# Top-64 attention on one Trainium2 core: the scan of candidates one step later, marks held twice, and GpSimd's pass over the scores

## The chip, the cores and the metric

The kernel runs on one core of one Trainium2 chip. The metric is device time in microseconds of one launch. The engines are TensorE (PE in the profile, PEld for its weight loads), VectorE (DVE), ScalarE (ACT), GpSimd (POOL) and SyncE (SP). A name with a q behind it (DVEq) is the sequencer of that engine, which handles waits, registers and branches.

## The reference

Sixteen batches of 512 rows of width 128 go through one layer of attention with 16 heads and a feed-forward layer. What matters here is the attention's choice of keys:

```
dots = einsum('bhid,bhjd->bhij', q, k) * scale     # 16 memory keys + 512 keys
dots = einsum('bhij,hk->bkij', dots, pre_proj)     # heads mixed
dots = where(causal, -max, dots)
vk   = top_k(dots, 64)[0][..., -1:]                # the 64th largest of each row
attn = softmax(where(dots < vk, -max, dots))
attn = einsum('bhij,hk->bkij', attn, post_proj)
out  = einsum('bhij,bhjd->bhid', attn, v) @ Wo + bo
x = x + layernorm(out);  x = x + layernorm(ffn(layernorm(x)))   # silu-gated ffn
```

## The kernel before

The kernel works in steps of one head of one batch: `step(s)` for s from 0 to 15, sixteen batches, and a "drain" batch at the end; a loop holds two batches. `g` counts the steps over all batches. A head's scores are four row tiles t = 3, 2, 1, 0 of 528, 400, 272 and 144 columns (only keys that the mask allows), 1344 columns in all, in one of 8 ring slots of `scores`.

To find the 64th largest value of each row, the kernel doesn't sort. It guesses a threshold, counts how many scores lie above it, moves the guess by a secant step, and repeats three times, once a step. A head goes through these stages, each on its own lag behind the step in which its scores are made:

- lag 0: TensorE makes the scores (L713 and L715, the causal mask added as a matmul); VectorE takes them out of PSUM (L1061, semaphore `masked`).
- lags 1, 2, 3: ScalarE counts with `Sign` (`count(k)`, L871, four tiles each, semaphore `counted[k]`). VectorE moves the three guesses in flight at once (the guess block, L1123 to L1149, semaphore `guess_ready`).
- lag 4 (`LAG_K`): VectorE counts a last time and writes marks 0 or 1 into `work` (`count_found`, L1014). It then writes score - FMAX * mark over them in one pass of 1344 columns (L1080), scans for the 8 largest that are left (MAX8, L1092) and picks the wanted one by its rank (`pick_rank` L1099 and `pick_value` L1107, semaphore `kth_ready`); GpSimd makes the table of ranks for that (`offset`, L1260, semaphore `offset_ready`). ScalarE takes the exponentials (L892). Rows for which the number found was too far off are counted (`spread` L1078, `missed` L1084, semaphore `bad_ready`).
- the flags: TensorE sums `missed` over partitions (L761, place ("FLAG", s) in the `misc` banks), ScalarE copies the sum to `flags` (L803, near the end of its step), and VectorE, one step later, loads it into a register (`value_load`, L1029). If it isn't zero, VectorE works out the tile concerned exactly (`general_kth`, L987 to L995).
- lag 5 (`LAG_P`): VectorE applies threshold and exponentials (L1048) and takes the reciprocal of the row sum (L1053, semaphore `rinv_ready`); GpSimd scales (L1269, `scaled`), TensorE transposes (L737, `turn`), ScalarE copies (L882, `take_turned`).
- lag 6 (`LAG_V`): TensorE weighs the values (L724).

Nothing is scheduled by a planner: each engine runs its own hand-written order and waits on semaphores. ScalarE's order in a step is `count(2)`, `count(1)`, `take_extra(0)`, the copy of G for the next head, `count(0)`, `take_extra(1)`, then the turned tiles between the exponentials, and the flag. The "extras" are projections, the feed-forward layer and the like, put into the steps by the table `EXTRAS`; their PSUM banks `misc` alternate, and `misc_free` counts every copy out of them in a fixed order. The two lines that tie the engines together around the change are, for ScalarE and VectorE:

```
L866  at_least(act, first_ready if k == 0 else guess_ready, g if k == 0 else g - 1)
L1028 dve.wait_ge(misc_free, flag_index(kind, b, s) + 1)   # ("FLAG", s - 1) has been copied
```

`guess_ready` goes up by one with each guess block. Before the change the block of VectorE's step g brings it to g, so `count` in ScalarE's step g (which wants g - 1) needs the block of step g - 1.

GpSimd's order in a step is `negmax` (L1249), the seed of a new guess (L1255), `offset` (L1260), the four scalings (L1269), `pmem` (L1276), the memory keys' scores (L1285), then its extras: layer norms (L1194 to L1204), residual sums (L1210) and a product of the feed-forward layer (L1307).

Of the kernel before, what the change touches and what calls it, by code (L numbers as in the profile page):

```python
# [41 lines left out]
MASKED = -2.0 ** 100  # L42
# [14 lines left out]
LAG_P = 5  # L57
LAG_V = 6
# [18 lines left out]
          4: [("U", 7), ("U", 8)],  # L77
          5: [("PM", 0), ("PM", 1)],
          6: [("U", 9), None],
          7: [("MEM", 0), ("MEM", 1)],  # L80
          8: [("U", 10), ("X1T",)],
          9: [("GATE", 0), ("UP", 0)],
          10: [("GATE", 1), ("UP", 1)],
          11: [("GATE", 2), ("UP", 2)],
          12: [("U", 11), ("U", 12)],
          13: [("DOWN", 0), ("DOWN", 1)],
          14: [("U", 13), ("U", 14)],
          15: [("U", 15), None]}
# [15 lines left out]
def guess_table():  # L104
# [23 lines left out]
    for t in range(T):  # L128
        for i in range(P):
# [4 lines left out]
            table[i, t] = z  # L134
            table[i, T + t] = z - FAR / (2 * density)
# [13 lines left out]
def flagged(kind, s):  # L149

    return lagged(kind, s, LAG_K)
# [120 lines left out]
def build(nc, table, x, wq, wk, wv, pre, post, memk, memv, wo, bo, wgate, wup, wdown, out):  # L272
    with ExitStack() as ctx:  # L273
# [12 lines left out]
        work = sb("work", [P, WIDE])  # L286
# [39 lines left out]
        found = sb("found", [P, T])  # L326
# [18 lines left out]
        minus_one = sb("minus_one", [P, T])  # L345
# [72 lines left out]
        found_ready = sem("found_ready")  # L418
        offset_ready = sem("offset_ready")
# [141 lines left out]
        def _(pe):  # L561
# [179 lines left out]
            def batch(kind, b, par):  # L741
                def step(s):
# [20 lines left out]
                    if lagged(kind, s, LAG_P):  # L763
                        turn(head_of(s, LAG_P), g - LAG_P, 2)
# [9 lines left out]
        def _(act):  # L774
# [20 lines left out]
            for q in range(4):  # L795
                nc.scalar.mul(a_all[:, 4 * q:4 * q + 4, :], banks[q][:, :].rearrange("p (h n) -> p h n", h=4),
                              DH ** -0.5).then_inc(a_taken, 1)
            nc.scalar.mul(amem[:, :, :], banks[4][:, 0:H * M].rearrange("p (h n) -> p h n", h=H),
                          DH ** -0.5).then_inc(a_taken, 1)
# [29 lines left out]
            def batch(kind, b, par):  # L829
                def step(s):  # L830
# [54 lines left out]
                    def exponentials(p):  # L885

                        if lagged(kind, s, LAG_K):
                            ge, t = g - LAG_K, ORDER[p]
# [3 lines left out]
                            nc.scalar.activation(row(expo, ring(head_of(s, LAG_K), ERING), t),  # L892
                                                 row(scores, ring(head_of(s, LAG_K), RING), t), ACT.Exp,
                                                 bias=negmax[:, bass.ds(ring(head_of(s, LAG_K), RING), 1), t]
# [31 lines left out]
        def _(dve):  # L926
# [76 lines left out]
            def batch(kind, b, par):  # L1003
                def step(s):
# [25 lines left out]
                    if selects:  # L1030
                        count_found(ORDER[2])
                        count_found(ORDER[3])
# [313 lines left out]
```

## Time and profile before

| what | us |
|---|---|
| median of 3 runs | 3636.93 (3633.64 to 3641.19) |
| the profiled execution's own time | 3636.07 |
| its span, first to last instruction | 3634.3 |
| VectorE busy | 3292.4 (91% of the span) |
| ScalarE busy | 3199.3 (88%) |
| TensorE matmuls busy | 2795.9 (77%) |
| GpSimd busy | 1551.4 (43%) |

The span is the time between the first and the last instruction in the trace; the profiled execution took 1.8 us more than its span. Busy time is the union of an engine's instructions; idle time is put down to what released the engine. One step takes some 13.5 us, and each engine does about the same in every step, so most of the reading is done on one step.

### The profile page before, as it was taken

How to read it: one execution, taken by the hardware profiler on the slowest of the kernel's cores; microseconds unless marked ns; L12 is line 12 of the kernel's file. 1: busy time of each engine (PE TensorE's matmuls, PEld its weight loads, DVE VectorE, ACT ScalarE, POOL GpSimd, SP SyncE). 2: the span in 40 equal slices, each digit the busy share in tenths (PEclk: the TensorE clock that was granted, in tenths of full speed). 3: DMA queues.
4: the chain of work that ended last, by engine and by line, in shares of the span. 5: the costliest groups of instructions: out<-in, count | busy, mean ns of one | idle time of the engine just before them, and what ended most of it. 6: DMA issues, size and time to landing. Idle time of an engine off the chain costs nothing. (4 is left out here: it accounts for less than half of the span.)

```text
span 3634.3 us, 67348 instructions
## 1 busy us (share of the span) xinstructions
PE 2795.9 (77%) x13751; PEld 1808.7 (50%) x13751; DVE 3292.4 (91%) x12492; ACT 3199.3 (88%) x9018; POOL 1551.4 (43%) x2663
## 2 busy tenths in 40 slices
PE   7777778777777878778778867877777788877765
PEld 3455455545545545555455545544555455545544
DVE  4699999999999999999999999999999999999994
ACT  1799999999979999999999979998999999999973
POOL 3233444444434444444444444443444444444433
PEclk9888999988888899888998888899889998899886
DMA  1000000000000000000000000000000000000000
GB/s 41 7 2 2 5 8 5 8 2 5 8 4 8 5 8 2 5 8 5 8 5 7 2 4 8 5 8 2 5 8 5 8 5 8 2 5 8 2 7 4
DMA packets 31375, 22.37 MB, mean 6 GB/s; under 512 B 3201, under 2 KB 30338, under 8 KB 30722
## 3 DMA queue, kind: packets, MB, share of 16 engines
q1 hardware_dynamic: 30722, 16.03, 1.6%
q14 instruction: 532, 4.36, 0.4%
q8 instruction: 121, 1.98, 0.2%
HBM read 11.83 MB, written 4.19 MB: 4 GB/s over the span
## 5 line engine op out<-in xcount | busy, mean ns | idle before, releaser
L871 ACT ACTIVATE signs<-scores,state 128x528 int8<-128x528 f32 (+3 forms) x3072 | 1764.3, 574 | 181.8 <-DVE state L1149 103.4
L713 PE MATMUL s_bank<-xn,gT 128*128 128x512 f32 (+3 forms) x2048 | 900.6, 568 | 1.7 <-issue 0.7
L1269 POOL TENSOR_SCALAR probs<-probs,rinv 128x528 f32<-128x528 f32 (+3 forms) x1024 | 547.1, 553 | 507.3 <-DVE rinv L1053 507.3
L737 PE MATMUL t_bank<-ident,probs 128*128 128x128 f32 x2560 | 482.7, 313 | 299.1 <-POOL probs L1269 289.7
L724 PEld LDWEIGHTS y_bank<-u_all,probsT 128*128 128x128 f32 x5120 | 619.9, 194 | 133.4 <-issue 124.2
L724 PE MATMUL y_bank<-u_all,probsT 128*128 128x128 f32 x5120 | 625.2, 278 | 7.1 <-ACT probsT L882 7.1
L1260 POOL TENSOR_TENSOR offset<-consts,found 128x36 f32<-128x36 f32 x256 | 161.7, 632 | 1047.5 <-DVE work L1014 1047.5
L871 ACT ACTIVATION_READ_ACCUMULATOR signs<-scores,state 128x1 f32 x3072 | 575.7, 187 | 0.0
L737 PEld LDWEIGHTS t_bank<-ident,probs 128*128 128x128 f32 x2560 | 299.7, 153 | 506.8 <-issue 398.6
L1048 DVE SCALAR_TENSOR_TENSOR probs<-scores,kth,expo 128x528 f32<-128x528 f32 (+3 forms) x1024 | 522.8, 565 | 24.8 <-issue 19.1
L892 ACT ACTIVATE expo<-scores,negmax 128x528 f32<-128x528 f32 (+3 forms) x1024 | 535.0, 575 | 0.0
L1014 DVE TENSOR_SCALAR_CACHE_REDUCE work<-scores,state 128x528 f32<-128x528 f32 (+3 forms) x1024 | 515.5, 559 | 20.2 <-issue 12.3
L1061 DVE TENSOR_SCALAR_CACHE_REDUCE scores<-s_bank,memmax 128x512 f32<-128x512 f32 (+3 forms) x1024 | 502.5, 547 | 3.8 <-PE s_bank L715 3.4
L713 PEld LDWEIGHTS s_bank<-xn,gT 128*128 128x128 f32 x2048 | 393.4, 239 | 222.4 <-issue 212.3
L882 ACT COPY probsT<-t_bank 128x512 f32<-128x512 f32 (+1 forms) x768 | 390.6, 509 | 104.5 <-PE t_bank L737 102.7
L1092 DVE MAX8 state<-work 128x8 f32<-128x528 f32 (+3 forms) x1024 | 444.9, 500 | 0.0
L1080 DVE SCALAR_TENSOR_TENSOR work<-work,scores 128x1344 f32<-128x1344 f32 x256 | 404.9, 1582 | 0.0
L599 PE MATMUL misc<-b_all,xn 128*128 128x512 f32 x512 | 281.3, 631 | 50.5 <-ACT u_all L803 46.3
L1276 POOL COPY pmem<-probs 128x64 f32<-128x64 f32 x256 | 303.5, 1186 | 35.9 <-issue 2.5
L761 PE MATMUL misc<-missed,onesP 128*1 128x5 f32 x512 | 49.4, 168 | 343.0 <-DVE missed L1084 340.0
L634 PE MATMUL misc<-xn,a_all 128*128 128x512 f32 x512 | 263.2, 596 | 0.0
L715 PE MATMUL s_bank<-causal,ident 128*128 128x128 bf16 x1024 | 250.5, 245 | 0.0
(148 smaller groups left out, 3384.9 us busy)
## 6 DMA issues: line engine op xcount, KB each, us to landing
xwork<-in_L_attn_x_dram SPq DMA_DIRECT2D x17, 256.0 KB, 2.8
xres<-in_L_attn_x_dram SPq DMA_DIRECT2D x16, 256.0 KB, 2.9
out_dram<-ybuf SPq DMA_DIRECT2D x16, 256.0 KB, 2.4
u_all<-in_L_attn_Wq_dram SPq DMA_DIRECT2D x1, 512.0 KB, 3.7
u_all<-in_L_attn_Wk_dram SPq DMA_DIRECT2D x1, 512.0 KB, 4.5
u_all<-in_L_attn_Wv_dram SPq DMA_DIRECT2D x1, 512.0 KB, 5.3
u_all<-in_L_attn_Wo_dram SPq DMA_DIRECT2D x1, 512.0 KB
expo<-in_L_ffn_w_gate_dram SPq DMA_DIRECT2D x1, 192.0 KB, 4.7
```

The source lines that it names most:

```text
L713: nc.tensor.matmul(score_part(t, 0, KEYS[t]), lhsT=gT[s % 2][:, t * P:(t + 1) * P], rhs=xn[par][:, 0:KEYS[t]], start=True, stop=False, ski ...
L724: mm = nc.tensor.matmul(y_bank[:, t * P:(t + 1) * P], lhsT=probsT[:, h % 2, at:at + P], rhs=u_all[:, j, h * D:(h + 1) * D], start=False, s ...
L737: mm = nc.tensor.transpose(t_bank[q % 2][:, at:at + P], probs[:, h % 2, KEY_AT[t] + j * P:KEY_AT[t] + (j + 1) * P], ident[:, :])
L871: nc.scalar.activation(signs[:, k, 0:ROW[t]], row(scores, ring(head_of(s, k + 1), RING), t), ACT.Sign, bias=guesses(s % STATES, k, GUESSES ...
L882: nc.scalar.copy(probsT[:, h % 2, PART_AT[q]:PART_AT[q + 1]], t_bank[q % 2][:, 0:PART_AT[q + 1] - PART_AT[q]]).then_inc(t_taken, 1)
L892: nc.scalar.activation(row(expo, ring(head_of(s, LAG_K), ERING), t), row(scores, ring(head_of(s, LAG_K), RING), t), ACT.Exp, bias=negmax[: ...
L1014: v.tensor_scalar(work[:, AT[t]:AT[t] + ROW[t]], row(scores, slot_k, t), guessed[:, t:t + 1], None, ALU.is_ge, ALU.add, accum_out=found[:, ...
L1048: v.scalar_tensor_tensor(out=probs[:, slot_p % 2, AT[t]:AT[t] + ROW[t]], in0=row(scores, slot_p, t), scalar=kth[:, bass.ds(slot_p, 1), t], ...
L1061: v.tensor_scalar(keys(scores, slot, t), score_part(t, 0, KEYS[t]), 1.0, memmax[par][:, t, bass.ds(s, 1)], ALU.mult, ALU.max, accum_out=ro ...
L1080: v.scalar_tensor_tensor(out=work[:, :], in0=work[:, :], scalar=-FMAX, in1=scores[:, bass.ds(slot_k, 1), :].squeeze(1), op0=ALU.mult, op1= ...
L1092: v.max(candidates(now)[:, t, 1:9], work[:, AT[t]:AT[t] + ROW[t]]).then_inc(select_step, 1)
L1269: nc.gpsimd.tensor_scalar(prb, prb, rinv[:, slot_p, t:t + 1], 1.0, ALU.mult, ALU.mult).then_inc(scaled, 1)
```

## The change

Three parts:

1. The lags. Applying moves from lag 5 to 6 (`LAG_P`), the values from 6 to 7 (`LAG_V`), the exponentials and flags get a lag of their own, 5 (`LAG_E`). The scan for candidates (MAX8) and the pick run one step after the marks were made; so `work` and `found` are held twice.
2. The pass over 1344 columns leaves VectorE. GpSimd does it as four subtractions, score - mark, one for each tile. So that a subtraction of 1 is enough to push a marked score under all others, all scores are scaled by 2^-60, and the scale is taken back in the exponential.
3. The order on VectorE. A step now begins with scan and pick, then the check of the number found, the feed-forward product, the guess block, one `count_found`, the applying, the other three `count_found`, and the scores out of PSUM. On ScalarE the flag comes after the last turned tile, on TensorE after the third `turn`.

```diff
-MASKED = -2.0 ** 100
+UNIT = 2.0 ** -60
+MASKED = -2.0 ** 40
...
 LAG_K = 4
-LAG_P = 5
-LAG_V = 6
+LAG_E = 5
+LAG_P = 6
+LAG_V = 7
...
-        work = sb("work", [P, WIDE])
+        work = sb("work", [P, 2, WIDE])
-        found = sb("found", [P, T])
+        found = sb("found", [P, 2, T])
...
 (TensorE)
                     if lagged(kind, s, LAG_P):
-                        turn(head_of(s, LAG_P), g - LAG_P, 0)
-                        turn(head_of(s, LAG_P), g - LAG_P, 1)
+                        for q in range(3):
+                            turn(head_of(s, LAG_P), g - LAG_P, q)
                     if flagged(kind, s):
-                        pe.wait_ge(bad_ready, g - LAG_K + 1)
+                        pe.wait_ge(bad_ready, g - LAG_E + 1)
...
-                    if lagged(kind, s, LAG_P):
-                        turn(head_of(s, LAG_P), g - LAG_P, 2)
...
 (ScalarE)
                     exponentials(2)
                     exponentials(3)
+                    take_turned(2)
                     if flagged(kind, s):
-                        at_least(act, probs_ready, 4 * (g - LAG_K))
+                        at_least(act, probs_ready, 4 * (g - LAG_E))
                         take(kind, b, par, ("FLAG", s), flags[:, :], ...)
-                    take_turned(2)
...
 (VectorE, at the start of a step)
+                    if applies:
+                        dve.wait_ge(hidden, 4 * gp + 4)
+                        alone(dve)
+                        for p, t in enumerate(ORDER):
+                            if p == 2:
+                                dve.wait_ge(misc_free, flag_index(kind, b, s) + 1)
+                                alone(dve)
+                                rows_missed = dve.value_load(flags[0:1, T:T + 1].bitcast(I32), ...)
+                            v.max(candidates(past)[:, t, 1:9], work[:, s % 2, AT[t]:AT[t] + ROW[t]]).then_inc(select_step, 1)
+                        dve.wait_ge(offset_ready, gp + 1)
...
                     if moves:
                         for k in range(GUESSES):
-                            if lagged(kind, s, k + 1):
-                                dve.wait_ge(counted[k], 4 * (g - k))
+                            if lagged(kind, s, k + 2):
+                                dve.wait_ge(counted[k], 4 * (g - k - 1))
...
-                        v.tensor_tensor(guesses(soon, 1, GUESSES), guess, move[:, :], ALU.subtract).then_inc(guess_ready, 1)
+                        v.tensor_tensor(guesses(now, 1, GUESSES), guess, move[:, :], ALU.subtract).then_inc(guess_ready, 1)
...
-                        v.scalar_tensor_tensor(out=work[:, :], in0=work[:, :], scalar=-FMAX,
-                                               in1=scores[:, bass.ds(slot_k, 1), :].squeeze(1),
-                                               op0=ALU.mult, op1=ALU.add).then_inc(select_step, 1)
...
 (GpSimd)
+                    if lagged(kind, s, LAG_K):
+                        gk, slot_k = g - LAG_K, ring(head_of(s, LAG_K), RING)
+                        for p, t in enumerate(ORDER):
+                            pool.wait_ge(found_ready, 4 * gk + p + 1)
+                            alone(pool)
+                            wrk = work[:, s % 2, AT[t]:AT[t] + ROW[t]]
+                            nc.gpsimd.tensor_tensor(wrk, row(scores, slot_k, t), wrk, ALU.subtract).then_inc(hidden, 1)
```

The wait of `count` on `guess_ready` (L866) isn't edited. The block of VectorE's step g now brings `guess_ready` to g - 1, since the first block runs one step later.

VectorE, in the middle of a batch, before: from the end of the guess block to the load of the flag (`candidates` are part of `state`, and `flags` holds what ScalarE copied in its last step).

```order
L1149 TENSOR_TENSOR state<-state,move 128x12
L1092 MAX state<-work 128x8 [waits select_step]
L1092 MAX state<-work 128x8 x3
L1099 SCALAR_TENSOR_TENSOR offset<-offset,state 128x4x9 [waits select_step,offset_ready]
L1106 ISA [waits select_step]
L1107 TENSOR_REDUCE kth<-offset 128x4
L1014 TENSOR_SCALAR work,found<-scores,state 128x528 [waits masked,guess_ready,mem_placed]
L1014 TENSOR_SCALAR work,found<-scores,state 128x400
L1029 TENSOR_LOAD flags [waits misc_free]
L1029 ISA x2
L1014 TENSOR_SCALAR work,found<-scores,state 128x272
L1014 TENSOR_SCALAR work,found<-scores,state 128x144
```

The same engine after the change, from the start of a step to the start of the guess block.

```order
L1031 MAX state<-work 128x8 [waits hidden]
L1031 MAX state<-work 128x8
L1029 TENSOR_LOAD flags [waits misc_free]
L1029 ISA x2
L1031 MAX state<-work 128x8 x2
L1034 SCALAR_TENSOR_TENSOR offset<-offset,state 128x4x9 [waits select_step,offset_ready]
L1038 ISA [waits select_step]
L1039 TENSOR_REDUCE kth<-offset 128x4
L1046 SCALAR_TENSOR_TENSOR spread<-found 128x4 [waits found_ready]
L1049 SCALAR_TENSOR_TENSOR missed<-spread,consts 128x4 [waits select_step]
L1069 TENSOR_TENSOR state<-counts,consts 128x12 [waits first_ready,counted2,counted0,counted1]
```

The load of the flag stood behind the guess block of the step before and some half a step ahead of the next one; it now stands directly ahead of a guess block, with two scans, the pick and the check between them.

ScalarE after the change, over the end of a step and the start of the next one.

```order
L883 COPY probsT<-t_bank 128x512 [waits t_full]
L893 ACTIVATE expo<-scores,negmax 128x272
L893 ACTIVATE expo<-scores,negmax 128x144
L880 REGISTER_ALU
L883 COPY probsT<-t_bank 128x256 [waits t_full]
L803 REGISTER_ALU [waits probs_ready]
L804 COPY flags<-misc 1x5 [waits misc_full]
L872 ACTIVATE signs,counts<-scores,state 128x528 [waits mem_placed,counted2,masked,guess_ready]
```

The copy of the flag was the last but one instruction of a step and is now the last; the next step still opens with `count(2)`, which waits for the guess.

GpSimd after the change, from the start of a step.

```order
L1237 TENSOR_TENSOR negmax<-rowmax,minus_unit 128x4 [waits masked]
L1243 COPY state<-seed 128x2x4 [waits guess_ready]
L1252 COPY scores<-smem 128x2x32 [waits probs_ready]
L1258 TENSOR_TENSOR offset<-consts,found 128x4x9 [waits kth_ready,found_ready]
L1268 TENSOR_SCALAR probs<-probs,rinv 128x528 [waits rinv_ready,probs_ready]
L1268 TENSOR_SCALAR probs<-probs,rinv 128x400
L1268 TENSOR_SCALAR probs<-probs,rinv 128x144
L1268 TENSOR_SCALAR probs<-probs,rinv 128x272
```

Behind these come the four subtractions and `pmem`, and then the extras; the memory keys' copy has moved ahead of `offset`.

## Rows read from the trace of the kernel before

**Rows 1.** The page, busy time and share of the span by engine.
```profile
PE 2795.9 (77%) x13751; PEld 1808.7 (50%) x13751; DVE 3292.4 (91%) x12492; ACT 3199.3 (88%) x9018; POOL 1551.4 (43%) x2663
```

**Rows 2.** VectorE's waits, 300 to 3500 us: total us, times, longest.
```profile
DVE state L1123 <- ACT signs L871: 0.4, 1, 0.4
```

**Rows 3.** ScalarE's groups, 500 to 3500 us: busy, mean ns, idle before by releaser.
```profile
L871 ACT ACTIVATE signs<-scores,state 128x272 int8<-128x272 f32 (+1 forms) x2667 | 1531.7, 574 | 156.4 <-DVE state L1149 88.1 <-issue 1.1
...
L882 ACT COPY probsT<-t_bank 128x512 f32<-128x512 f32 (+1 forms) x666 | 339.0, 509 | 64.4 <-PE t_bank L737 63.1
L803 ACT COPY gT<-misc 128x512 f32<-128x512 f32 x223 | 130.9, 587 | 5.7 <-PE misc L634 5.7
```

**Rows 4.** Timeline of VectorE, one step: start us, duration us.
```profile
2013.38 0.43 DVE L1078 SCALAR_TENSOR_TENSOR spread<-found 128x4 f32<-128x4 f32 x1
2013.73 1.55 DVE L1080 SCALAR_TENSOR_TENSOR work<-work,scores 128x1344 f32<-128x1344 f32 x1
2015.20 0.19 DVE L1084 SCALAR_TENSOR_TENSOR missed<-spread,consts 128x4 f32<-128x4 f32 x1
...
2015.32 0.25 DVE L1123 TENSOR_TENSOR state<-counts,consts 128x12 f32<-128x12 f32 x1
...
2017.16 1.74 DVE L1092 MAX8 state<-work 128x8 f32<-128x528 f32 x4
2019.01 0.22 DVE L1099 SCALAR_TENSOR_TENSOR offset<-offset,state 128x36 f32<-128x36 f32 x1
2019.37 0.20 DVE L1107 TENSOR_REDUCE kth<-offset 128x4 f32<-128x40 f32 x1
```

**Rows 5.** Timeline of ScalarE, the end of the same step and the next.
```profile
2016.86 0.14 ACT L803 COPY flags<-misc 1x5 f32<-1x5 f32 x1
2016.91 0.37 ACT L882 COPY probsT<-t_bank 128x256 f32<-128x256 f32 x1
2017.28 0.73 ACT L871 ACTIVATE signs<-scores,state 128x528 int8<-128x528 f32 x1
```

**Rows 6.** Timeline of VectorE and ScalarE while the pipeline fills.
```profile
132.60 0.17 DVE L1123 TENSOR_TENSOR state<-counts,consts 128x12 f32<-128x12 f32 x1 [6.92 <-ACT signs L871]
...
134.27 0.17 DVE L1149 TENSOR_TENSOR state<-state,move 128x12 f32<-128x12 f32 x1
134.48 0.73 ACT L871 ACTIVATE signs<-scores,state 128x528 int8<-128x528 f32 x1 [1.53 <-DVE state L1149]
134.62 0.76 DVE L1014 TENSOR_SCALAR_CACHE_REDUCE work<-scores,state 128x528 f32<-128x528 f32 x1 [0.17 <-DVE state L1149]
```

**Rows 7.** Line 1029, the load of the flag: ns min/median/max.
```profile
L1029 DVEq TENSOR_LOAD <-flags x256: 302/306/552, 148.1 to 3580.4; - x128
L1029 DVEq FUSED_REGOPS  x256: 183/199/203, 148.7 to 3580.8; - x128
```

**Rows 8.** GpSimd: two stretches of its timeline and one group by shape.
```profile
2011.69 2.10 POOL L1269 TENSOR_SCALAR probs<-probs,rinv 128x528 f32<-128x528 f32 x4 [2.33 <-DVE rinv L1053]
2013.93 1.45 POOL L1276 COPY pmem<-probs 128x64 f32<-128x64 f32 x1
...
2215.08 0.24 POOL L1276 COPY pmem<-probs 128x64 f32<-128x64 f32 x1
...
2216.07 1.44 POOL L1194 TENSOR_SCALAR vareps<-meanvar 128x4 f32<-128x4 f32 x1 [0.58 <-DVE meanvar L962]
...
2221.21 1.27 POOL L1210 TENSOR_TENSOR ybuf<-xres,ybuf 128x512 f32<-128x512 f32 x1
...
L1307 POOL TENSOR_TENSOR f_up<-f_up,f_gate 128x512 f32<-128x512 f32 x48 | 61.6, 1283 | 8.8 <-ACT f_up L803 8.8
```

**Rows 9.** VectorE's product of the feed-forward layer, by shape.
```profile
L1165 DVE SCALAR_TENSOR_TENSOR f_up<-f_tanh,f_up 128x512 f32<-128x512 f32 x48 | 33.1, 690 | 17.4 <-POOL f_up L1307 15.2 <-issue 2.2
```

**Rows 10.** Timeline behind one `general_kth`: VectorE applies, GpSimd scales.
```profile
2156.32 0.77 DVE L1048 SCALAR_TENSOR_TENSOR probs<-scores,kth,expo 128x528 f32<-128x528 f32 x1 [0.15 <-DVE kth L995]
...
2158.77 2.10 POOL L1269 TENSOR_SCALAR probs<-probs,rinv 128x528 f32<-128x528 f32 x4 [17.97 <-DVE rinv L1053]
```

More of the change, by code:

```diff
@@ L133, in guess_table @@
             active = n + M > TOPK
[L134 to L135 removed]
+            table[i, t] = z * UNIT ** 0.5
+            table[i, T + t] = (z - FAR / (2 * density)) * UNIT ** 0.5
             table[i, 5 * T + 9 * T + t] = float(active)
@@ L149, in flagged @@
 def flagged(kind, s):
-    return lagged(kind, s, LAG_K)
+    return lagged(kind, s, LAG_E)
 def makes_g(kind, s):
@@ L418, in build @@
         found_ready = sem("found_ready")
+        hidden = sem("hidden")
         offset_ready = sem("offset_ready")
@@ L1006, in step @@
                     v = nc.vector
-                    slot_k, slot_p = ring(head_of(s, LAG_K), RING), ring(head_of(s, LAG_P), RING)
-                    gk, gp = g - LAG_K, g - LAG_P
-                    selects, applies = lagged(kind, s, LAG_K), lagged(kind, s, LAG_P)
-                    moves = any(lagged(kind, s, k + 1) for k in range(GUESSES))
-                    now, soon, past = s % STATES, (s + 1) % STATES, (s - 1) % STATES
-                    def count_found(t):
-                        v.tensor_scalar(work[:, AT[t]:AT[t] + ROW[t]], row(scores, slot_k, t), guessed[:, t:t + 1],
-                                        None, ALU.is_ge, ALU.add, accum_out=found[:, t:t + 1]).then_inc(found_ready, 1)
+                    slot_k, slot_e, slot_p = [ring(head_of(s, lag), RING) for lag in (LAG_K, LAG_E, LAG_P)]
@@ new lines, in step @@
+                    gk, ge, gp = g - LAG_K, g - LAG_E, g - LAG_P
+                    selects, checks, applies = [lagged(kind, s, lag) for lag in (LAG_K, LAG_E, LAG_P)]
+                    moves = any(lagged(kind, s, k + 2) for k in range(GUESSES))
+                    now, last, past = s % STATES, (s - 1) % STATES, (s - 2) % STATES
+                    def count_found(t):
+                        v.tensor_scalar(work[:, s % 2, AT[t]:AT[t] + ROW[t]], row(scores, slot_k, t), guessed[:, t:t + 1],
+                                        None, ALU.is_ge, ALU.add,
+                                        accum_out=found[:, s % 2, t:t + 1]).then_inc(found_ready, 1)
@@ new lines, in step @@
+                    if checks:
+                        number = found[:, (s - 1) % 2, :]
+                        dve.wait_ge(found_ready, 4 * ge + 4)
+                        alone(dve)
+                        v.scalar_tensor_tensor(out=spread[:, :], in0=number, scalar=-2.0 * AIM, in1=number,
+                                               op0=ALU.add, op1=ALU.mult).then_inc(select_step, 1)
+                        dve.wait_ge(select_step, 1)
+                        v.scalar_tensor_tensor(out=missed[:, 0:T], in0=spread[:, :], scalar=WINDOW ** 2 + 0.5 - AIM ** 2,
+                                               in1=active, op0=ALU.is_gt, op1=ALU.mult,
+                                               accum_out=missed[:, T:T + 1]).then_inc(bad_ready, 1)
@@ L1053, in step @@
                         v.reciprocal(rinv[:, slot_p % 2, :], rowsum[:, :]).then_inc(rinv_ready, 1)
+                    if selects:
+                        for t in ORDER[1:]:
+                            count_found(t)
                     if kind != "drain":
@@ L1063, in step @@
                                             accum_out=rowmax[:, bass.ds(slot, 1), t]).then_inc(masked, 1)
-                    if s == 6 and kind != "first":
+                    if s == 0 and kind in ("first", "mid"):
+                        dve.wait_ge(x_in, 16 * (b + 2))
+                        norm_stats(kind, b, "x", xwork)
+                    if s == 8 and kind in ("first", "mid"):
+                        memory_maxima(kind, b, 1 - par)
+                    if s == LAG_V and kind != "first":
```

229 lines of the change are left out of this document (99 added, 130 removed).

## The prediction

> **What bounds the kernel now.** I read the page's shares first: VectorE is busy for 91% of the span and ScalarE for 88%, GpSimd for 43% [rows 1]. Then the waits: from 300 to 3500 us VectorE waits for ScalarE's counts 0.4 us in all [rows 2], so it runs nearly without a pause and sets the pace. ScalarE from 500 to 3500 us makes 223 steps (one copy of G each), which is 3000 / 223 = 13.45 us a step; it waits 88.1 us for guesses, 63.1 us for turned tiles and 5.7 us for G [rows 3]. Without these 157 us its step would take (3000 - 157) / 223 = **12.75 us**. So ScalarE is the next bound, 0.7 us behind VectorE.
>
> Last the timelines, for what stands in series. Before the change VectorE's guess block of step g waits for the counts of ScalarE's step g and serves its step g + 1. ScalarE meanwhile does its extras, exponentials and turned tiles. In the step shown the block begins at 2015.32, and ScalarE begins to count at 2017.28, right behind its last copy [rows 4, 5]. The flag, copied at 2016.86, is wanted only in VectorE's next step, ahead of a guess block that serves the step after that. So the loop through the flag spans two steps and doesn't bind.
>
> **The change, part by part.**
>
> The pass over 1344 columns leaves VectorE: 2015.20 - 2013.73 = 1.47 us a step [rows 4]. With it goes a wait at `spread`, which takes 0.43 us there for four columns. If VectorE still set the pace this would give up to 1.7 us, of which only 13.45 - 12.75 = 0.7 us is to be had before ScalarE binds. I book nothing of it, for the next part.
>
> **The flag's wait now stands inside a loop of one step.** In the new order VectorE's step g scans two tiles, waits until ScalarE has copied the flag of step g - 1, loads it, scans two more tiles, picks, checks, and only then runs its guess block. That block now works on the counts of step g - 1 and brings `guess_ready` to g - 1, which is the very value that the first count of ScalarE's step g waits for. And the flag is now the last thing that ScalarE does in a step. So ScalarE ends step g - 1, stands still until VectorE has gone from the flag's load to the end of the guess block, and begins step g. The period is ScalarE's whole step plus this link, whatever VectorE has saved. The link, piece by piece:
> - flag copied to load issued: 0.04 us, as between the end of the guess (134.27 + 0.17) and ScalarE's start at 134.48 [rows 6];
> - the load 0.31 and the register work 0.20, with the assertion behind it 0.55 [rows 7]. Now it stands hidden behind running counts; in the new place nothing is queued, so all of it shows. Bounds: 0.3 (the load alone) and 0.8 (load and register work start 0.6 us apart in the first instance, then 0.2);
> - 0.07 to the scan, then the scans of 272 and 144 columns. Four scans take 1.74 us [rows 4]; by columns the two would be 416 / 1344 of that, 0.54, and half of it would be 0.87. I take 0.64, nearer to the columns, as most of an instruction's time grows with them;
> - scan's end (2017.16 + 1.74) to pick 0.11, taken as 0.10, pick to threshold 0.36 (2019.01 to 2019.37), and 0.23 for the threshold up to the next instruction [rows 4];
> - check: 0.21 for `spread` (bounded by 0.12 and by the 0.35 from 2013.38 to 2013.73), and 0.12 from `missed` at 2015.20 to the guess block [rows 4];
> - the guess block 1.84, from 132.60 to 134.44, and 0.04 to ScalarE [rows 6].
>
> Sum: 0.04 + 0.55 + 0.07 + 0.64 + 0.10 + 0.36 + 0.23 + 0.21 + 0.12 + 1.84 + 0.04 = **4.20 us**, with 3.8 and 5.0 as bounds.
>
> The load, by its rows, isn't slow. The Trainium skill (DMA: Bandwidth & Descriptors, Latency and other measured facts) gives a `tensor_load` a floor of some 600 ns. The rows show 302 ns at least, so they speak against it; by the page the sum would be 0.3 us a step, some 75 us in all, longer.
>
> ScalarE's step itself grows by 0.09: the flag's 0.14 us overlapped the turned tile (2016.86 to 2016.91) and now ends the step [rows 5]. 12.75 + 0.09 = 12.84. I expect no other wait in it. GpSimd begins to scale some 3.5 us after a step's guess, and ScalarE wants the first turned tile behind three counts, 1531.7 / 223 = 6.9 us without their gaps [rows 3], and three copies: some 9 us after it. The two extra slots and G are as before. TensorE has 17 us for what now takes it 2796 / 256 = 10.9 at most. Its wait for `missed` goes, and costs nothing either way.
>
> GpSimd's step. The pass: a product of two tiles of 512 columns takes 1.28 us [rows 8], 2.5 ns a column, so 1344 columns are 3.4 us, with gaps of 0.12 3.85 us (bounds: 2.1 us, the price of the four one-operand scalings, and 5). Counted from the guess's end: VectorE goes on at 0.18 [rows 6], counts one tile (0.7, and 0.2 to the next), applies and takes the reciprocal, and GpSimd starts to scale 2.45 us after the applying began [rows 10], at 3.5; it scales until 5.65, passes until 9.5, copies `pmem` until 9.85. `pmem` takes 0.24 us instead of 1.45, since the latter was a wait beside VectorE's pass [rows 8]. Four small operations lead to `offset` at 11.1. VectorE wants it at 12.84 + 0.04 + 0.55 + 0.07 + 0.64 + 0.10 = 14.2: hidden, with 3 us to spare. Behind the extras it isn't. The norm with residual takes some 5.2 us (2216.07 to 2222.48, less the 1.2 by which its first operation was held up) [rows 8]; it puts `offset` at 16.3, 2.1 us late, twice a batch. The norm without the residual, 1.3 us shorter, makes it 0.8 us late, twice. That is 5.8 us a batch, 0.36 us a step; bounds 0 and 0.8. The feed-forward product on VectorE (0.69 us, three times a batch [rows 9]) now stands between flag and guess: 0.13 us a step.
>
> `general_kth` runs four times as before (the scale is a power of two). It delays the scaling by some 16 us (GpSimd waits 17.97 instead of 2 [rows 8, 10]). Scaling begins at 3.5 and the turned tile is wanted at 9, with a tile's scaling and turning between, so about 5 us of it hide in ScalarE's step now, and it costs three times 11 and once, for a narrow tile, 5: 38 us. The old pace of 13.45 holds such stalls already; I add the 38 nevertheless, since the new pace is without any.
>
> **Sum.** Period 12.84 + 4.20 + 0.36 + 0.13 = **17.53 us**, against 13.45: 4.08 more. The loop closes from step 6 of the first batch into the fourth step of the drain, 253 times: 253 x 4.08 = 1032. With 38: 1070. The profiled execution took 3636.1 us by itself, a microsecond from the median of 3636.9; 3636 + 1070 = 4706, and I write **4700 us**. The lag that the values gain falls into the drain, which has spare steps; I book nothing for it.
>
> **The rivals.**
>
> *The pass comes late or collides.* If GpSimd's loop (scaling, pass, `offset`, pick, guess, applying) were the longer one, it would decide. It takes 11.1 to `offset` against 14.2, so it decides once the pass takes over 7 us. For it: GpSimd and VectorE do hold each other up, as `pmem` (1.45 for 0.24) beside VectorE's pass and `spread` (0.43) beside the last scaling show [rows 4, 8]. Against it: from 5.65 to 9.5 VectorE does counts, evictions and scans, then waits for the flag; the small operations with two operands lie behind 14.2, when GpSimd is idle. The Trainium skill (SBUF - State Buffer, Who interferes with whom) has the rule: a VectorE instruction with two SBUF inputs and a GpSimd instruction that reads SBUF exclude each other. By that rule the pass is undisturbed here. With a pass of 9 us the period would be 2 us longer: 4700 + 506 = 5200 us.
>
> *The flag doesn't bind, GpSimd does.* If the change didn't close the loop as I read it (the flag's wait met early), GpSimd's loop would set the pace: 11.1 to `offset`, and 0.36 + 0.23 + 0.21 + 0.12 + 1.84 = 2.8 plus 0.2 back to the guess's end, 14.1 us. Its extras, 22 us a batch (twice 5.2, twice 3.9, three times 1.3), add 1.4: 15.5 us, 3636 + 253 x 2.05 = 4155 us. Against it: the wait for the flag of step g - 1 is met by one copy alone, since `misc_free` counts in a fixed order.
>
> *Faster.* VectorE's saved pass counts in full, and ScalarE runs without a pause at 12.84 us: 3636 - 253 x 0.61 = 3480 us. Its place is ScalarE's first count of a step; it decides only if the link shrinks to under 0.6 us, or the guess comes a step ahead, and if GpSimd's loop stays under 12.8. The rows speak against both: the guess block alone takes 1.84.
>
> **How the numbers follow.** My forecast, the loop through the flag, gets 0.92; the late pass 0.02, GpSimd's loop without the flag 0.03, not slower 0.03. The range: link at 3.8, no lateness of `offset` and no stalls give 12.75 + 3.8 + 0.13 = 16.7 us, 4455; link at 5.0 and lateness 0.8 give 18.8 us, 5027. All unknowns at one end together are unlikely; half way to the ends holds 8 in 10: 4570 to 4880. A measurement of this kernel tells 0.2% from no change. So faster by more than that 0.02 and within it 0.01, which share the 0.03 of the rival above, and slower 0.97, the other three.
>
> **What would show it.** ScalarE idles some 4.2 us before its first `Sign` of nearly every step, released by the last instruction of the guess block, and hardly elsewhere; its busy time is as before. VectorE idles some 4 to 5 us between the second and the third MAX8 of a step, its busy time lower by some 400 us, 256 passes of 1.55. The link from flag to first `Sign` is 4.2 us. GpSimd's four subtractions take 3.4 us, `pmem` 0.24, `spread` under 0.2; GpSimd idles before the scaling. TensorE no longer waits for `missed`. It would be wrong if ScalarE ran from the flag straight into the count, if the pass met VectorE's small operations, or if VectorE waited mostly for `offset`.

## The result, and the profile after

The changed kernel takes 4640.84 us (median of four executions), the kernel before 3638.12 us beside it: a ratio of 1.276, with a 95% interval from 1.273 to 1.278. The forecast was 4700 us, in a range from 4570 to 4880. One of the four executions took 7459.95 us, at a granted clock of 1.0; it is left out of the ratio, and what happened in it stays open.

The page of the changed kernel, span and shares [rows 1 before]:

```profile
span 4638.8 us, 70407 instructions
...
PE 3121.9 (67%) x13751; PEld 2029.2 (44%) x13751; DVE 2789.2 (60%) x12236; ACT 3188.9 (69%) x9018; POOL 1980.1 (43%) x3687
```

VectorE lost 503 us of work, ScalarE kept its own, and no engine is busy for 70% of the span any more. When all shares fall and the time grows, the time lies in waits. These are the longest of each of the three engines, 500 to 4500 us (total us, times, longest) [rows 2, 3 before]:

```profile
ACT signs L872 <- DVE state L1095: 1047.5, 229, 9.7
ACT probsT L883 <- PE t_bank L740: 29.2, 10, 11.2
ACT smem L804 <- PE misc L645: 10.0, 8, 1.5
...
DVE state L1031 <- ACT flags L804: 1231.2, 228, 6.6
...
DVE offset L1034 <- POOL offset L1258: 34.0, 22, 5.5
...
POOL probs L1268 <- DVE rinv L1124: 2236.2, 230, 26.2
```

In 229 steps ScalarE waits 229 times for the end of the guess block (L1095), 4.57 us each, and VectorE 228 times for the flag, 5.4 us each. Each waits for the other, once a step. The timeline shows one turn of the loop: ScalarE's first count of a step, the end of that step, the link (VectorE's work from the flag to the end of the guess block), and the first count of the next step [rows 4 to 6 before]:

```profile
2501.34 0.73 ACT L872 ACTIVATE signs<-scores,state 128x528 int8<-128x528 f32 x1 [5.03 <-DVE state L1095]
...
2507.75 1.19 DVE L1031 MAX8 state<-work 128x8 f32<-128x528 f32 x2
...
2513.58 0.37 ACT L883 COPY probsT<-t_bank 128x256 f32<-128x256 f32 x1
2513.83 0.15 ACT L804 COPY flags<-misc 1x5 f32<-1x5 f32 x1
2514.72 0.66 DVE L1031 MAX8 state<-work 128x8 f32<-128x272 f32 x2 [5.78 <-ACT flags L804]
2515.49 0.22 DVE L1034 SCALAR_TENSOR_TENSOR offset<-offset,state 128x36 f32<-128x36 f32 x1
2515.85 0.19 DVE L1039 TENSOR_REDUCE kth<-offset 128x4 f32<-128x40 f32 x1
2515.96 0.16 DVE L1046 SCALAR_TENSOR_TENSOR spread<-found 128x4 f32<-128x4 f32 x1
2516.16 0.16 DVE L1049 SCALAR_TENSOR_TENSOR missed<-spread,consts 128x4 f32<-128x4 f32 x1
...
2516.37 0.17 DVE L1069 TENSOR_TENSOR state<-counts,consts 128x12 f32<-128x12 f32 x1
...
2518.04 0.17 DVE L1095 TENSOR_TENSOR state<-state,move 128x12 f32<-128x12 f32 x1
2518.24 0.74 ACT L872 ACTIVATE signs<-scores,state 128x528 int8<-128x528 f32 x1 [4.26 <-DVE state L1095]
```

ScalarE works from 2501.34 to 2513.98, 12.64 us. Then VectorE alone works until 2518.21, and ScalarE starts at 2518.24: a link of 4.26 us. VectorE had been done with its first two scans at 2508.94 and stood still for 5.78 us.

GpSimd in the same step [rows 8 before]:

```profile
2504.92 2.10 POOL L1268 TENSOR_SCALAR probs<-probs,rinv 128x528 f32<-128x528 f32 x4 [10.07 <-DVE rinv L1124]
2506.99 3.47 POOL L1276 TENSOR_TENSOR work<-scores,work 128x528 f32<-128x528 f32 x4
2510.39 0.25 POOL L1283 COPY pmem<-probs 128x64 f32<-128x64 f32 x1
...
2511.03 0.26 POOL L1258 TENSOR_TENSOR offset<-consts,found 128x36 f32<-128x36 f32 x1
```

The pass takes 3.47 us and ends before the flag is there.

### The profile page after: what moved, and what is told of

It is laid out like the page before. It is cut to its first block and busy times, and to the rows that moved or that the text cites. A ratio compares the mean times of both kernels' runs of the same rounds, so it can differ in the third digit from the quotient of the medians.

```text
span 4638.8 us, 70407 instructions
## 1 busy us (share of the span) xinstructions
PE 3121.9 (67%) x13751; PEld 2029.2 (44%) x13751; DVE 2789.2 (60%) x12236; ACT 3188.9 (69%) x9018; POOL 1980.1 (43%) x3687
## 5 line engine op out<-in xcount | busy, mean ns | idle before, releaser
L1031 DVE MAX8 state<-work 128x8 f32<-128x528 f32 (+3 forms) x1024 | 472.2, 506 | 1376.0 <-ACT flags L804 1363.5
L716 PE MATMUL s_bank<-xn,gT 128*128 128x512 f32 (+3 forms) x2048 | 944.2, 589 | 5.9 <-ACT gT L804 4.2
L740 PE MATMUL t_bank<-ident,probs 128*128 128x128 f32 x2560 | 589.5, 385 | 465.0 <-ACT probsT L883 290.2
L1276 POOL TENSOR_TENSOR work<-scores,work 128x528 f32<-128x528 f32 (+3 forms) x1024 | 886.0, 897 | 16.4 <-DVE work L1017 16.4
L602 PE MATMUL misc<-b_all,xn 128*128 128x512 f32 x512 | 381.2, 835 | 622.6 <-ACT u_all L804 480.0
L740 PEld LDWEIGHTS t_bank<-ident,probs 128*128 128x128 f32 x2560 | 451.5, 201 | 747.3 <-issue 352.0
L727 PE MATMUL y_bank<-u_all,probsT 128*128 128x128 f32 x5120 | 649.2, 285 | 10.2 <-ACT probsT L883 10.2
L602 PEld LDWEIGHTS misc<-b_all,xn 128*128 128x128 f32 x512 | 98.0, 240 | 664.8 <-ACT u_all L804 499.6
L696 PE MATMUL misc<-x1T,wgT 128*128 128x512 f32 x96 | 88.6, 1021 | 215.0 <-ACT f_up L804 138.7
L718 PEld LDWEIGHTS s_bank<-causal,ident 128*128 128x128 bf16 x1024 | 117.6, 115 | 159.3 <-issue 133.7
```

What stands on the lines that cost most here:

```text
L602: nc.tensor.matmul(misc[misc_place(kind, par, ("U", u))][:, :], lhsT=xn[par][:, (u % 4) * P:(u % 4 + 1) * P], rhs=b_all[:, 4 * (u // 4):4 ...
L716: nc.tensor.matmul(score_part(t, 0, KEYS[t]), lhsT=gT[s % 2][:, t * P:(t + 1) * P], rhs=xn[par][:, 0:KEYS[t]], start=True, stop=False, ski ...
L727: mm = nc.tensor.matmul(y_bank[:, t * P:(t + 1) * P], lhsT=probsT[:, h % 2, at:at + P], rhs=u_all[:, j, h * D:(h + 1) * D], start=False, s ...
L740: mm = nc.tensor.transpose(t_bank[q % 2][:, at:at + P], probs[:, h % 2, KEY_AT[t] + j * P:KEY_AT[t] + (j + 1) * P], ident[:, :])
L1031: v.max(candidates(past)[:, t, 1:9], work[:, s % 2, AT[t]:AT[t] + ROW[t]]).then_inc(select_step, 1)
L1276: nc.gpsimd.tensor_tensor(wrk, row(scores, slot_k, t), wrk, ALU.subtract).then_inc(hidden, 1)
```

## The experiments

Theory A in all of them: the loop from the flag through VectorE's link to ScalarE's count sets the pace. The rivals are named in each expectation. The edits are made to the changed kernel; `LOAD` stands for the wait on `misc_free`, the nop and the `value_load` of the flag.

**1. The load behind all four scans.**

```diff
                         for p, t in enumerate(ORDER):
-                            if p == 2: LOAD
                             v.max(...)
+                        LOAD
                         dve.wait_ge(offset_ready, gp + 1)
```

> The changed kernel, with VectorE's wait for the flag and its load put behind all four scans instead of between the second and the third. Theory A, the loop through the flag: the two small scans leave the link between flag and guess. In the changed kernel's timeline they and the gap before the pick take 0.66 + 0.1 us, so a step gets some 0.7 us shorter: 4641 - 253 x 0.7 = 4460 us, and ScalarE's idle time before its first count falls from 4.6 to 3.9 us a step. Theory B, GpSimd sets the pace (scaling, pass, ranks): nothing of its chain moves, 4641 us. Theory C, TensorE's lower granted clock (0.79 against 0.88) makes the time: no change, 4641 us.

Measured: 4493.26 us. In plain steps ScalarE's wait is 3.56 us, which is the 4.26 less 0.70:

```profile
1953.95 0.73 ACT L872 ACTIVATE signs<-scores,state 128x528 int8<-128x528 f32 x1 [3.56 <-DVE state L1094]
```

The pick now starts 0.81 us behind the end of the flag's copy, and it was 1.51 us (2513.98 to 2515.49): the same 0.70 us have left the link. The time fell by 148 us and not by 180. Over all steps from 500 to 3500 us ScalarE's wait fell from 4.60 to 4.06 us, by 0.54, since in some steps GpSimd's ranks now come last, after the flag. VectorE's waits that ended with the ranks, over the whole run, changed kernel and this one:

```profile
DVE offset L1034 <- POOL offset L1258: 36.1, 24, 5.5
DVE offset L1033 <- POOL offset L1257: 313.1, 63, 6.0
```

The 313 us are whole waits, most of which would have gone to the flag in any case; what counts is that 63 steps end on the ranks, and it was 24. Theory A holds; B and C, which saw no change, fall.

**2. The flag early.** TensorE sums the flag ahead of the three `turn`s, ScalarE copies it behind `take_extra(1)`.

```diff
                     take_extra(1)
+                    if flagged(kind, s): at_least(...); take(kind, b, par, ("FLAG", s), ...)
                     take_turned(0)
...
                     take_turned(2)
-                    if flagged(kind, s): at_least(...); take(kind, b, par, ("FLAG", s), ...)
```

> The changed kernel, with the flag summed by TensorE ahead of the turned tiles and copied by ScalarE behind its second extra, some 3.1 us earlier in its step; VectorE's order is untouched. Theory A: ScalarE's start to the end of the flag is then 9.6 us, and with a link of 4.26 us the loop through the flag takes 13.9 us instead of 17.5. The steps in which GpSimd does its norms are longer, since its own chain (offset 10 us after ScalarE's start, then 2.8 us to the end of the guess, plus 5.2 us for a norm with residual, 3.9 for one without) comes next: 0.85 us a step on average. 14.75 us against 13.45 before: 3638 + 253 x 1.3 = 3970 us. Theory B: 4641 us, as GpSimd's order is the same. Theory C: 4641 us.

Measured: 4035.04 us. Nothing on VectorE or GpSimd has moved, no work was saved, and 606 us are gone: a copy of 0.15 us, and the matmul that feeds it, had only to come earlier. That is 65 us more than the 3970 expected. A plain step, from count to count in the rows below, is shorter than expected, 13.40 us for 13.9, but the mean is 3000 / 199 = 15.1 us: the steps with GpSimd's norms cost more than the 0.85 us a step booked for them. 63 of VectorE's waits now end on the ranks (500 to 3500 us):

```profile
1948.88 0.74 ACT L872 ACTIVATE signs<-scores,state 128x528 int8<-128x528 f32 x1 [1.19 <-DVE state L1095]
1962.28 0.74 ACT L872 ACTIVATE signs<-scores,state 128x528 int8<-128x528 f32 x1 [1.18 <-DVE state L1095]
...
DVE offset L1034 <- POOL offset L1258: 185.8, 63, 5.9
```

**3. The load late.** `missed` is held twice here, since the wait for the flag had also kept it from being written again too early.

```diff
-                            if p == 2: LOAD
...
                         count_found(ORDER[0])
                     if applies:
+                        LOAD
                         dve.wait_ge(exp_ready, 4 * gp + 4)
```

> The changed kernel, with the wait for the flag and its load behind the guess block and the first count, just ahead of the applying; missed is held twice, so that the earlier wait isn't needed to protect it. Theory A: the flag no longer stands ahead of the guess, the link is gone. What is left is ScalarE's 12.8 us, and GpSimd's chain of 12.7 us in a plain step and 21 us of extras a batch: 14.2 us a step at most, 3638 + 253 x 0.73 = 3820 us, and 3480 us if the extras hide. Theory B: GpSimd's chain is the same, 4641 us. Theory C: 4641 us.

Measured: 4087.31 us. The loop through the flag is open, and the time is far from 3820. The waits say what stands there instead (total us, times, longest, 500 to 3500 us):

```profile
ACT signs L872 <- DVE state L1090: 488.4, 196, 9.2
...
DVE offset L1029 <- POOL offset L1257: 541.5, 195, 5.9
DVE probs L1118 <- issue: 208.1, 201, 3.4
```

VectorE waits in 195 of 196 steps for GpSimd's ranks, which stand behind pass and norms. This is the second rival of the prediction, the GpSimd loop without the flag, to which it gave 15.5 us a step and 4155 us; 3000 / 196 = 15.3 us are measured. The expectation of 3820 had left out what the last row shows: the load, with nothing queued ahead of it, now shows in front of the applying, 1.0 us a step, and that is a piece of GpSimd's loop.

That the rival's 15.5 us come so near is in part luck. From the guess's end at 2000.73 the ranks are ready 10.92 us later here, where it had 11.1; but 1.0 us of that is the load, which it had not counted, and its GpSimd pieces were some 1.1 us too long (worked out below).

**4. The ranks early.** GpSimd makes the ranks one step before they are used, from the same counts.

```diff
-                    if lagged(kind, s, LAG_P):
-                        at_least(pool, kth_ready, g - LAG_P)
-                        pool.wait_ge(found_ready, 4 * (g - LAG_P) + 4)
+                    if lagged(kind, s, LAG_E):
+                        at_least(pool, kth_ready, g - LAG_E)
+                        pool.wait_ge(found_ready, 4 * (g - LAG_E) + 4)
...
-                                                found[:, s % 2, :]...
+                                                found[:, (s - 1) % 2, :]...
```

> The changed kernel, with GpSimd's table of ranks made one step earlier, ahead of the scaling, so that neither the pass nor the norms stand ahead of it; the flag's wait is untouched. Theory A: the loop through the flag is untouched, only the 34 us in which VectorE waited for the ranks (500 to 4500 us) go: 4605 us. Theory B: the pass leaves GpSimd's loop, some 5 us a step: ScalarE's pace, 3500 us. Theory C: 4641 us.

Measured: 4617.75 us, 23 us less. As long as the loop through the flag is closed, taking the pass out of GpSimd's loop is worth half a per cent. Theory B falls for the changed kernel.

**5. Early flag and early ranks together**, VectorE's order untouched.

> The early flag with GpSimd's ranks a step earlier, VectorE's order untouched. It shows the loop through the flag alone, with the flag 3.1 us earlier. Theory A: 9.6 us from ScalarE's start to the end of the flag and 4.26 us of link make 13.9 us, plus 0.13 us for the feed-forward product: 14.0 us, 3634 + 253 x 0.6 = 3785 us, and ScalarE idles about 1.2 us a step. Theory B: no gain against the 4035 us of the early flag alone.

Measured: 3930.98 us. In the plain step looked at, the flag ends at 2012.86 and the next count starts at 2017.12:

```profile
2003.76 0.74 ACT L872 ACTIVATE signs<-scores,state 128x528 int8<-128x528 f32 x1 [1.18 <-DVE state L1095]
2012.72 0.14 ACT L804 COPY flags<-misc 1x5 f32<-1x5 f32 x1
2017.12 0.73 ACT L872 ACTIVATE signs<-scores,state 128x528 int8<-128x528 f32 x1 [1.19 <-DVE state L1095]
```

9.10 + 4.26 = 13.36 us: the same link of 4.26 us in a kernel that is 700 us faster, behind a flag that comes 3.5 us earlier. The plain step is shorter than expected. But the steps with norms take 15.5 to 16.6 us, so the mean is 3000 / 205 = 14.6 us and not 14.0, and the time is 146 us over the 3785 expected. In the step of 16.6 us `offset`, `spread` and the first operation of the guess block took 1.00, 0.78 and 0.98 us on VectorE, beside GpSimd's norm, where they take 0.22, 0.16 and 0.17 us in the changed kernel. The next run shows the same in more detail.

**6. Late load and early ranks together.** Both loops are open.

> The two edits of the last experiments together: VectorE's load of the flag behind the guess block (with missed held twice), and GpSimd's ranks made a step earlier, ahead of the scaling. Theory A (two loops stood behind one another: first the flag's, 17.5 us a step, then GpSimd's, 15.3 us): both are open now, and the next bound is ScalarE without waits, 12.75 to 12.85 us against 13.45 before: 3634 - 253 x 0.65 = 3470 us, 0.95 of before. Theory B (the pass on GpSimd or its scheme as such costs time by load, not by its place in a loop): not under 3900 us. Theory D (VectorE becomes the bound again, since its load of the flag shows 0.8 us a step and its work is 10.7 us): it has 1.3 us to spare in a plain step, so the same 3470 us, or 3550 us if its norms (1.4 to 2.7 us) don't hide.

Measured: 3682.00 us, ratio 1.013 (1.011 to 1.015). Against the 4087 us of the late load alone the early ranks are now worth 405 us, and 23 us while the flag's loop was closed. But 3470 us isn't reached, nor 3550. ScalarE still waits for the guess 182.8 us (111 times, 500 to 3500 us): in the stretches looked at, mostly 1.4 to 6 us in a step with a norm, less in the steps behind it, and 0.6 to 1.2 us in the three steps of a batch with the feed-forward product. VectorE and GpSimd in a step with a norm:

```profile
2016.01 0.87 DVE L959 BATCH_NORM_STATS2 stats<-ybuf 128x6 f32<-128x128 f32 x4
2017.01 0.38 DVE L964 BATCH_NORM_AGGREGATE meanvar<-stats 128x2 f32<-128x6 f32 x4
2018.04 1.75 DVE L1026 MAX8 state<-work 128x8 f32<-128x528 f32 x4 [0.64 <-POOL work L1275]
...
2020.55 1.04 POOL L1187 TENSOR_TENSOR ybuf<-ybuf,meanvar 128x512 f32<-128x512 f32 x1
2020.66 0.95 DVE L1044 SCALAR_TENSOR_TENSOR missed<-spread,consts 128x4 f32<-128x4 f32 x1
...
2021.74 1.08 POOL L1191 TENSOR_TENSOR ybuf<-ybuf,rstd 128x512 f32<-128x512 f32 x1
2021.96 0.91 DVE L1072 SCALAR_TENSOR_TENSOR between<-product,between 128x24 f32<-128x24 f32 x1
...
2022.97 1.26 POOL L1197 TENSOR_TENSOR ybuf<-xres,ybuf 128x512 f32<-128x512 f32 x1
2023.12 1.15 DVE L1082 TENSOR_TENSOR apart<-state 128x24 f32<-128x24 f32 x1
```

Operations of VectorE that take 0.16 to 0.18 us in the changed kernel take 0.91 to 1.15 us here. Each ends where the GpSimd operation beside it ends: at 2021.61, 2022.87 and 2024.27, and GpSimd's at 2021.59, 2022.82 and 2024.23. Between the two counts of 528 columns on VectorE, from 2008.76 to 2025.59, lie 16.8 us. The three held-up instructions are 2.5 us of that; 1.4 us are the norm's statistics on VectorE itself, 0.64 us a wait for a pass that comes late, and 1.2 us the load in the open, which stands in the plain steps too. The Trainium skill (SBUF - State Buffer, Who interferes with whom) states that a VectorE instruction with two SBUF inputs and a GpSimd instruction that reads SBUF contend for a pair of ports that only one of them can hold. These rows agree: VectorE's instructions waited, and GpSimd's took 1.04, 1.08 and 1.26 us, for 1.04, 1.04 and 1.27 on the mean in the changed kernel.

**7. All three edits.**

> All three edits: load behind the guess, early flag, early ranks. Theory A: ScalarE is the bound in either case, so nothing more than with two edits: 3470 us, within 10 us of the run with two. Theory D (the flag's wait, now ahead of the applying, still costs): some 0.5 us a step less than with two edits, 120 us.

Measured: 3664.16 us, 18 us less than with two. Between the two expectations, nearer to the first.

**8. Counts first.** Late load and early ranks, and the other three counts moved ahead of the applying, with the load between the second and the third, where it stood before the change.

```diff
                         count_found(ORDER[0])
+                        count_found(ORDER[1])
                     if applies: LOAD
+                    if selects: count_found(ORDER[2]); count_found(ORDER[3])
                     if applies: ...
-                    if selects:
-                        for t in ORDER[1:]: count_found(t)
```

> The kernel with two edits (late load, early ranks), with all four last counts ahead of the applying again and the load of the flag between the second and the third, as in the kernel before. In the run with two edits VectorE stood 250 us (500 to 3500 us) before the applying for the load, 1.1 us a step, and steps with a norm took 17 us. Theory D (VectorE is the bound in the steps with a norm, ScalarE in the plain ones): the load hides behind counts; a norm step gets some 1.1 us shorter, a plain one not: 4 to 7 of 16 steps, 70 to 130 us: 3682 - 100 = 3580 us. Theory A alone (ScalarE the bound everywhere): 3682 us, no change.

Measured: 3622.57 us, ratio 0.995 (0.994 to 0.997). VectorE's idle time ahead of the applying, with two edits and here (500 to 3500 us):

```profile
DVE probs L1118 <- issue: 250.3, 224, 3.7
DVE probs L1122 <- issue: 33.7, 78, 3.4
```

The time fell by 59 us. That speaks for theory D and against "no change", but it lies under the 70 to 130 us that D gave.

**9. Counts first with the early flag.**

> The same with the early flag. It took 18 us off with the load in the open; with the load hidden behind counts both theories see the flag met long before: within 20 us of the run without it, some 3565 us by theory D, which would be 2% under the kernel before, and the candidate for a version faster than both.

Measured: 3594.07 us, ratio 0.987 (0.986 to 0.989): 1.3% faster than the kernel before, and 29 us over the 3565 expected. The early flag is worth 28.5 us here, more than the 20 at which the expectation had put its limit. What the kernel loses shows in a plain step. With the applying later and the step shorter, GpSimd's pass (2011.90 to 2015.37) reaches into the pick and the check:

```profile
2011.90 3.47 POOL L1275 TENSOR_TENSOR work<-scores,work 128x528 f32<-128x528 f32 x4
...
2013.33 0.94 DVE L1029 SCALAR_TENSOR_TENSOR offset<-offset,state 128x36 f32<-128x36 f32 x1
2014.53 0.41 DVE L1041 SCALAR_TENSOR_TENSOR spread<-found 128x4 f32<-128x4 f32 x1
2014.97 0.42 DVE L1044 SCALAR_TENSOR_TENSOR missed<-spread,consts 128x4 f32<-128x4 f32 x1
```

In the changed kernel these took 0.22, 0.16 and 0.16 us, so the pass costs VectorE 1.2 us in this step, of the 1.47 that it took as VectorE's own. On the mean of 225 steps the three take 0.80, 0.35 and 0.36 us, 0.95 us a step more than in the changed kernel.

**10. A quarter of the norms.** The last kernel, with three quarters of GpSimd's work in three norms of a batch left out: it centres, scales and adds one row tile of four, so its output isn't the layer's.

> The same as the last, but GpSimd centres, scales and adds only the first of four row tiles in the norms of the attention's output, of the sum and of the feed-forward output (the norm of x is whole), so three quarters of that work are left out. Theory E (GpSimd's long reading operations hold up VectorE's small two-operand block: 0.9 to 1.15 us for operations that take 0.18, three times in the step looked at, and GpSimd is late with the pass): the three norm steps lose 3 us each or more, 16 x 3 x 3 = 140 us less than the whole norms: some 3430 us. Theory F (those steps are long because of VectorE's own statistics and the waits for ScalarE): under 40 us less.

Measured: 3534.41 us, 60 us less than with whole norms. That lies between theories E and F: 1.2 us for each of 48 norms. GpSimd's long operations do cost there, and less than the step looked at suggests. ScalarE's waits for the guess, with whole norms and with a quarter (500 to 3500 us):

```profile
ACT signs L872 <- DVE state L1090: 117.5, 66, 4.3
ACT signs L872 <- DVE state L1090: 71.2, 58, 4.3
```

VectorE's thirteen small two-operand instructions from pick to guess take 3.62 us a step with whole norms and 3.40 with a quarter, by their means, which is some 56 us over the run. VectorE waits for the pass ahead of its scans 3.7 us in either kernel, so a late pass isn't what the norms cost. That the rest of the 3 us expected for a norm is made good in the plain steps behind is likely, but not shown.

## Why the prediction was right

**The loop through the flag.** Right, and it carries the result: in each of 229 steps ScalarE stands still for the guess. Taking 0.70 us out of the link took 0.70 us off the wait of a plain step; making and copying the flag earlier, with nothing else changed, took 606 us off.

**The link of 4.20 us.** Measured 4.26. From the flag's end to the first scan behind the load it is 0.74 us, forecast as 0.04 + 0.55 + 0.07 = 0.66; the two scans 0.66 for 0.64; from the pick's start at 2515.49 to the guess block at 2516.37 it is 0.88 for 0.92, and from there to ScalarE's count 1.87 for 1.88. The load itself is as before:

```profile
L1029 DVEq TENSOR_LOAD <-flags x256: 301/307/547, 157.1 to 4583.8; - x128
```

The floor of about 600 ns that the Trainium skill gives (DMA: Bandwidth & Descriptors, Latency and other measured facts) doesn't hold here; the load took 301 ns at least and 307 in the median, and the sum from the rows was right. No row ahead of the prediction shows the 0.07 us from the load to the scan, or the assertion in the 0.55; behind the wait all of it together takes 0.74 us.

**ScalarE's step of 12.84 us.** From 500 to 4500 us: (4000 - 1047.5 - 29.2 - 10.0) / 229 = 12.72 us. The 0.09 us for the flag at the end was not there on the mean.

**GpSimd's step.** Counted from the guess's end at 2501.30, scaling starts at 3.62 (forecast 3.5), the pass ends at 9.16 (9.5), `pmem` at 9.34 (9.85) and `offset` at 9.99 (11.1). The pass takes 3.47 us for 3.4 by columns; the gaps between its four operations, which I had put at 0.12 us each, don't show. The larger part of the error lies behind `pmem`: the small operations that lead to `offset` take 0.65 us and were put at 1.25, since they overlap (2510.57 to 2511.29). This was the term with the largest error: the lateness behind norms is 34.0 us in 229 steps, 0.15 us a step, and was put at 0.36. `pmem` takes 0.25 us and `spread` 0.16, as forecast.

**VectorE's busy time.** It fell by 503 us, and 400 were forecast. The pass was 256 x 1.57 = 403 us of it. The forecast had left out that VectorE's small two-operand instructions stood beside GpSimd's operations in the kernel before, and no longer do. Two of them, 500 to 3500 us before and 500 to 4500 us after:

```profile
L1128 DVE TENSOR_TENSOR product<-state 128x24 f32<-128x24 f32 x222 | 83.8, 378 | 0.0
L1078 DVE SCALAR_TENSOR_TENSOR spread<-found 128x4 f32<-128x4 f32 x222 | 82.3, 371 | 0.0
...
L1074 DVE TENSOR_TENSOR product<-state 128x24 f32<-128x24 f32 x229 | 41.9, 183 | 0.0
L1046 DVE SCALAR_TENSOR_TENSOR spread<-found 128x4 f32<-128x4 f32 x229 | 37.3, 163 | 1.8 <-issue 1.8
```

**The sum.** The period is 4000 / 229 = 17.47 us, against 17.53. Piece by piece it is 12.72 for ScalarE's work, 4.26 for the link, 0.15 for late ranks, 0.13 for the feed-forward product, and 0.18 for ScalarE's other waits, of which the forecast had none in its period: 17.44. So the nearness of 17.47 to 17.53 is in part luck: the ranks' lateness and ScalarE's step were put 0.33 us too high together, and the link and the other waits 0.24 too low. (The range as written, 4570 to 4880, is a little wider than half way to its ends, 4578 to 4864; the result lies in either.) 253 x (17.47 - 13.45) = 1017 us; the two profiled executions lie 4640.6 - 3636.1 = 1004.5 us apart. The forecast of 1070 was 65 us too high, and 38 us of that are the stalls of `general_kth`, which were added on top of a difference of means: the old pace holds stalls too, so at least most of this was counted twice.

**The rivals.** The pass never met VectorE's small operations in the changed kernel, as forecast: from 500 to 4500 us the longest `offset`, `spread` and `missed` took 0.230, 0.166 and 0.165 us. The GpSimd loop without the flag was priced at 4155 us, and the kernel with the late load, which is that case but for the load in the open, took 4087. "Faster" was priced at 3480 us, ScalarE without a pause; with both loops open, the load hidden and the flag early it is 3594 us. That price had left out that a faster step brings the pass and the norms of GpSimd into VectorE's two-operand block.

## What to carry to other kernels

When an edit moves a wait, follow what is released behind it round to whoever signals it, and count the pipeline steps on the way. If it is one, the period is the sum of all pieces on that round, whatever the engines' busy time says; a copy of 0.15 us at the end of one engine's step tied 4.3 us of another engine's work into every step here, and making and copying the flag earlier gave back 606 us. Loops like this hide one another: the same edit (the early ranks) was worth 23 us while the longer loop was closed and 405 us when it was open.

Work that is handed to a second engine isn't free because that engine idles: the pass lengthened none of VectorE's instructions as long as it stood beside one-operand work, and in the step shown 1.2 of its 1.5 us came back when a shorter step pushed it into the small two-operand instructions. It can also stand in a loop of its own engine: with the late load its 3.45 us were part of what set the pace.

## What the hardware showed that I had not expected

The length of a held-up VectorE instruction was set by its neighbour and not by its own size: 4 or 24 columns took 0.91 to 1.15 us beside GpSimd operations of 1.04 to 1.26 us, and ended within 0.05 us of them. I had expected some of that for the pass, and not for the norms.

TensorE's granted clock fell from a mean of 0.884 to 0.787 in the changed kernel, in which TensorE's matmuls fill 67% of the span instead of 77%, and with all loops open it was 0.908. Its busy time grew from 2795.9 to 3121.9 us with the same 13751 matmuls. No experiment tells what the lower clock depends on, and ScalarE's waits for TensorE, 39 us of 4000, show that it cost next to nothing here.
